# Query and key projections of the first attention as three fp16 products instead of one fp32 product

## The reference

```
x = x + attn(layernorm(x))                  # B=2, S=1024, E=128, H=16, D=64
Q = x @ Wq[h] + bq ; K = x @ Wk[h] + bk     # 128 columns a head: two halves of 64
V = x @ Wv[h] + bv                          # 64 columns a head
A1 = Q1 K1^T / 8 ; A2 = Q2 K2^T / 8         # 1024 x 1024, two of them a head
P  = softmax(A1) - lam * softmax(A2)
O  = P V ; Y = concat(O) @ Wo + bo ; Y = layernorm(Y) * gamma + beta, times 0.2
```

## Time and profile before

| what | value |
|---|---|
| median of 3 runs | 1667.67 us (1665.87 to 1667.73) |
| the profiled execution | 1667.55 us, span of its core 1665.8 us |
| TensorE matmul busy | 1543.7 us, 93% of the span |
| VectorE busy | 1316.4 us, 79% |
| ScalarE busy | 1266.0 us, 76% |
| GpSimd busy | 976.0 us, 59% |

### The profile page before, as it was taken

How to read it: one execution, slowest core, us unless ns; L and a number is a source line. 1 busy time by engine, 2 the same in 40 slices (tenths; PEclk the granted TensorE clock), 3 DMA queues, 4 the chain that set the end, 5 groups by cost and what they waited for, 6 DMA issues and landing times.

```text
span 1665.8 us, 27976 instructions
## 1 busy us (share of the span) xinstructions
PE 1543.7 (93%) x10479; PEld 641.2 (38%) x10479; DVE 1316.4 (79%) x2043; ACT 1266.0 (76%) x2039; POOL 976.0 (59%) x655
## 2 busy tenths in 40 slices
PE   5899999999999999999999999997575999999985
PEld 2444444444444444444444444434452222222223
DVE  6687887778877787878877788778958989999946
ACT  4788888888888888888888888884531888888872
POOL 2798887888878888788888888782022000111111
PEclk9999999999999999999999999998777999999997
DMA  4010011100111011110111111100001110000001
GB/s 125 20 34 24 22 28 25 37 23 23 28 34 28 24 26 25 34 26 23 29 23 34 28 23 26 26 19 6 1 12 29 27 34 15 16 15 16 15 15 32
DMA packets 51055, 43.67 MB, mean 26 GB/s; under 512 B 26101, under 2 KB 39322, under 8 KB 50922
## 3 DMA queue, kind: packets, MB, share of 16 engines
q1 hardware_dynamic: 50922, 41.90, 10.2%
HBM read 20.27 MB, written 1.31 MB: 13 GB/s over the span
## 4 chain that ended last, share of the span: by engine, by line
PE 76%; issue 9%; DVE 8%; ACT 4%; POOL 2%; DMA 1%; SPq 1%; POOLq 0%; ACTq 0%; DVEq 0%
PE PS L1500 22%; PE PS L1512 17%; PE PS L1524 14%; PE PS L1885 4%; PE PS L1567 4%; PE PS L1548 3%; PE PS L1848 2%; PE PS L1869 2%; PE PS L1584 2%; PE PS L1538 2%; DVE mxp L1406 2%; ACT ering L998 1%; ACT ering L786 1%; PE PS L1898 1%; POOL on L703 1%
## 5 line engine op out<-in xcount | busy, mean ns | idle before, releaser
L1091 DVE TENSOR_REDUCE nmx<-PS 128x1 f32<-128x1024 f32 x512 | 622.0, 1220 | 181.9 <-PE PS L1501 181.6
L606 POOL TENSOR_TENSOR ering<-ering 128x1024 f32<-128x1024 f32 x256 | 604.0, 2359 | 21.3
L786 ACT ACTIVATE ering<-PS,nmx 128x1024 f32<-128x1024 f32 x512 | 570.4, 1114 | 47.2 <-DVE nmx L1091 46.0
L1500 PE MATMUL PS<-region 64*128 64x512 f16 x1536 | 404.9, 381 | 7.2 <-DMA region<-region 5.3
L604 POOL TENSOR_SCALAR ering<-ering,rho 128x1024 f32<-128x1024 f32 x256 | 287.6, 1123 | 203.0 <-DVE rho L1100 200.5
L1501 PE MATMUL PS<-region 64*128 64x512 f16 x1536 | 404.9, 381 | 0.0
L1512 PE MATMUL PS<-ident,ering 128*128 128x128 f32 x2048 | 335.0, 286 | 8.8 <-ACT t L797 6.4
L1406 DVE TENSOR_REDUCE mxp<-PS 128x2 f32<-128x1024 f32 x256 | 304.1, 1221 | 41.7 <-PE PS L1869 38.1
L998 ACT ACTIVATE ering<-PS 128x1024 f32<-128x1024 f32 x256 | 260.4, 1025 | 74.2 <-PE PS L1848 66.6
L1512 PEld LDWEIGHTS PS<-ident,ering 128*128 128x128 f32 x2048 | 215.6, 141 | 260.7 <-issue 222.7
L1500 PEld LDWEIGHTS PS<-region 64*128 64x128 f16 x1536 | 112.6, 94 | 250.4 <-ACT ering L786 73.0
(11 more groups left out here) (289 smaller groups left out, 1800.1 us busy)
## 6 DMA issues: line engine op xcount, KB each, us to landing
region<-region SPq DMA_DIRECT2D x64, 256.0 KB, 3.5
osb<-scr SPq DMA_DIRECT2D x32, 128.0 KB, 3.1
rcp<-scr SPq DMA_DIRECT2D x32, 128.0 KB, 3.1
rcp<-scr SPq DMA_DIRECT2D x64, 64.0 KB, 2.0
region<-region SPq DMA_DIRECT2D x9, 128.0 KB, 2.6
x<-in_L_attn_X SPq DMA_DIRECT2D x4, 256.0 KB, 3.3
wq_raw<-in_L_attn_Wq SPq DMA_DIRECT2D x16, 64.0 KB, 3.2
wk_s<-in_L_attn_Wk SPq DMA_DIRECT2D x16, 64.0 KB, 1.9
```

The costliest lines, as they stand in the source:

```text
L606: P.tensor_tensor(e1, e1, e2, ALU.subtract).then_inc(s_sub_ok, 1)
L786: A.activation((E1, E2)[p][s % 4], PS[:, bank:bank + 2, :].rearrange("p a b -> p (a b)"), ACT.Exp, bias=nmx[:, 2 * s + p:2 * s + p + 1], s ...
L1091: V.tensor_reduce(nmx[:, 2 * s + p:2 * s + p + 1], PS[:, bank:bank + 2, :].rearrange("p a b -> p (a b)"), AX.X, ALU.max, negate=True).then ...
L1500: MM(PS[:, bank, :], top[0:64, ql, q], KT[b][0:64, p, kl, :], start=(j == 0), stop=(j == 2))
```

## The change

From the second head on (turn index `m >= 2`), Q and K are projected as three fp16 products (high x high, weights high x tokens low, weights low x tokens high) summed in PSUM, instead of one fp32 product. GpSimd makes the parts: of the transposed tokens once, in slots 1 to 4 of turn 0 (`part_x`), and of both weight matrices once a head (`part_w`), in slot 4 of every even turn, where `scale_q` now goes too (it was in slot 6). TensorE waits for the parts (`s_wlo_ok`, `s_xlo_ok`). The load of the next `wk_s` waits for the parts instead of for TensorE's products, from the second load on. Turns 0 and 1 are projected as before.

```diff
+        xs = sb("xs", [128, 2, N], F16)
+        wqh, wkh = [r16(15360 + 256 * i, 256).rearrange("p (l c) -> p l c", l=2) for i in range(2)]
...
+        PRODUCTS = ((0, 0), (0, 1), (1, 0))
...
                 if own and b == 0 and h + 1 < H0:
-                    sp.wait_ge(s_k0_mm, 2 * (n + 2))
+                    if h == 0:
+                        sp.wait_ge(s_k0_mm, 2 * (n + 2))
+                    else:
+                        sp.wait_ge(s_wlo_ok, h)
                     sp.dma_start(wk_s[:, :], a["L0_attn_Wk"][h + 1]).then_inc(s_ld_wk, 16)
...
+            def part_w(h):
+
+                scale_q(h)
+                pool.wait_ge(s_wqs_ok, h + 1)
+                pool.wait_ge(s_ld_wk, 16 * (h + 1))
+                pool.wait_ge(s_k0_mm, 4 * h)
+                P.tensor_copy(wqh[:, 0, :], wq_s[:, :])
+                P.tensor_copy(wkh[:, 0, :], wk_s[:, :]).then_inc(s_whi_ok, 1)
+                pool.wait_ge(s_whi_ok, h)
+                P.tensor_tensor(wqh[:, 1, :], wq_s[:, :], wqh[:, 0, :], ALU.subtract)
+                P.tensor_tensor(wkh[:, 1, :], wk_s[:, :], wkh[:, 0, :], ALU.subtract).then_inc(s_wlo_ok, 1)
+
+            def part_x(i):
+
+                at = slice(HF * i, HF * i + HF)
+                pool.wait_ge(s_xt_ev, i + 1)
+                P.tensor_copy(xs[:, 0, at], xT[:, at]).then_inc(s_xhi_ok, 1)
+                pool.wait_ge(s_xhi_ok, i + 1)
+                P.tensor_tensor(xs[:, 1, at], xT[:, at], xs[:, 0, at], ALU.subtract).then_inc(s_xlo_ok, 1)
...
             def prepare(n, s):
 
+                if n == 0 and 1 <= s < 5:
+                    part_x(s - 1)
...
-                    if s == 6 and b == 0 and h + 1 < H0:
-                        scale_q(h + 1)
+                    if s == 4 and b == 0 and h + 1 < H0:
+                        part_w(h + 1)
...
             def project_q(m):
 
-                pe.wait_ge(s_wqs_ok, m // 2 + 1)
+                if m < 2:
+                    pe.wait_ge(s_wqs_ok, 1)
+                else:
+                    pe.wait_ge(s_wlo_ok, m // 2)
+                    pe.wait_ge(s_xlo_ok, 4)
                 if m >= 1:
                     pe.wait_ge(s_exp, 16 * (m - 1) + 3)
                 for i in range(2):
-                    at = m % 2 * T + i * HF
-                    mm = MM(PS[:, Q_PAIR + i, :], wq_s[:, :], xT[:, at:at + HF], start=True, stop=True)
+                    at = slice(m % 2 * T + i * HF, m % 2 * T + i * HF + HF)
+                    dst = PS[:, Q_PAIR + i, :]
+                    if m < 2:
+                        mm = MM(dst, wq_s[:, :], xT[:, at], start=True, stop=True)
+                        continue
+                    for j, (wl, xl) in enumerate(PRODUCTS):
+                        mm = MM(dst, wqh[:, wl, :], xs[:, xl, at], start=(j == 0), stop=(j == 2))
                 mm.then_inc(s_q_mm, 1)
 
             def project_k(m, part):
 
-                pe.wait_ge(s_ld_wk, 16 * (m // 2 + 1))
+                if m < 2:
+                    pe.wait_ge(s_ld_wk, 16)
+                else:
+                    pe.wait_ge(s_wlo_ok, m // 2)
+                    pe.wait_ge(s_xlo_ok, 4)
...
-                for c in range(2):
-                    at = m % 2 * T + c * HF
-                    mm = MM(dst[64 * c:64 * c + 64, :], wk_s[:, 64 * part:64 * part + 64], xT[:, at:at + HF],
-                            start=True, stop=True)
+                d = slice(64 * part, 64 * part + 64)
+                for j, (wl, xl) in enumerate(PRODUCTS[0:1] if m < 2 else PRODUCTS):
+                    for c in range(2):
+                        at = slice(m % 2 * T + c * HF, m % 2 * T + c * HF + HF)
+                        if m < 2:
+                            mm = MM(dst[64 * c:64 * c + 64, :], wk_s[:, d], xT[:, at], start=True, stop=True)
+                        else:
+                            mm = MM(dst[64 * c:64 * c + 64, :], wkh[:, wl, d], xs[:, xl, at], start=(j == 0),
+                                    stop=(j == 2))
                 mm.then_inc(s_k0_mm, 1)
```

More of the change, by code:

```diff
@@ L190, in two_layers @@
         s_wqs_ok = sem("s_wqs_ok")
+        s_whi_ok = sem("s_whi_ok")
+        s_wlo_ok = sem("s_wlo_ok")
+        s_xhi_ok = sem("s_xhi_ok")
+        s_xlo_ok = sem("s_xlo_ok")
         s_fill = sem("s_fill")
@@ L1498, in scores @@
                 q = slice(s * 128, s * 128 + 128)
-                for j, (ql, kl) in enumerate(((0, 0), (0, 1), (1, 0))):
+                for j, (ql, kl) in enumerate(PRODUCTS):
                     MM(PS[:, bank, :], top[0:64, ql, q], KT[b][0:64, p, kl, :], start=(j == 0), stop=(j == 2))
```

## The result

The changed kernel took 1642.88 us (median of 4 runs, 1640.82 to 1644.57) against 1667.7 before: a ratio of 0.9849, 95% interval 0.9829 to 0.9868. In three later comparisons, each with its own runs of the kernel before, the same kernel took 1644.04, 1644.45 and 1645.10 us, ratios 0.9866 (0.9853 to 0.9880), 0.9885 (0.9870 to 0.9899) and 0.9866 (0.9851 to 0.9882). So the gain is 19 to 25 us, and the first median the lowest of four; the forecast of 20.1 lies in that span, and the three later medians lie inside the range. The turns say more than the medians: their length repeats within 0.02 us.

A forecast was written before the change was run, and what follows sets the result against it. TensorE was taken to bound the kernel. A turn loses 0.26 (second K product) + 0.41 (Q) = 0.67 us; 30 turns give 20.1 us, so 1667.55 - 20.1 = 1647.4 us, range 1643 to 1654.

The forecast's parts named there:

- the first K product: K's first half in slot 0: its 0.26 us saving becomes a wait for VectorE, so worth nothing.
- GpSimd at nothing: Making the parts delays tile 5 by 1.2 us with 2.1 us to spare, so costs nothing.
- rival (a): The first K product counts too, VectorE's chain moving with it: 27.9 us saved, 1639.7 us; chance 0.09.
- The second K product: K's second half, after the wait for VectorE: fp16 saves 0.26 us a turn, counted in full.
- Q: Q's projection as six fp16 passes, 1.40 us instead of 1.81: saves 0.41 us a turn, counted in full.
- rival (c): Weight loads no longer hide behind the shorter fp16 passes: turns 0.14 us longer, 1671.8 us; chance 0.05.
- The cap at 0.74: A turn cannot lose more than about 0.74 us, where ScalarE's chain alone sets the pace.
- SyncE at nothing: The next K weights load earlier and no longer hold the swap of Q; effect nothing.
- (b): Only Q counts; VectorE's and ScalarE's chain takes the second K product's gain: 12.3 us saved, 1655.3 us; chance 0.07.
- (d): GpSimd's fp16 casts are several times dearer, each head pays 1.9 us: 28 against 20.1 us, 1676 us; chance 0.03.

The follow-up runs named there:

- e3: Changed kernel with only the first half of K projected in fp32 again; 1642.71 us, turns of 33.70 us.
- e14: Changed kernel with the addition to the output cut to 16 columns and the first half of K in fp32 again; 1644.02 us, turns of 33.70 us.
- e13: Changed kernel with the addition to the output cut to 16 columns, first half of K left in fp16; 1640.91 us, turns of 33.53 us.
- e5: Changed kernel with only the second half of K projected in fp32 again; 1648.41 us, turns of 33.85 us.
- e4: Changed kernel with only Q projected in fp32 again; 1654.44 us, turns of 34.03 us.
- e8: Changed kernel with V also projected as three fp16 products, from the second pair of heads on; 1644.55 us, turns of 33.61 us.
- e2: Changed kernel with GpSimd making all parts but TensorE projecting in fp32; 1663.28 us, ratio 0.9984 against the kernel before, turns of 34.36 us.
- e6: Changed kernel with the third product of Q (low part of its weights) left out; 1635.09 us, turns of 33.42 us.

## Why the prediction was wrong, and where it was right

The step that failed is the one that put the first K product at nothing. It gave 0.09 us a turn, 2.7 us of the 4.7 by which the forecast was short. The rest of the working held: two of three terms to within 0.03 us, and GpSimd at nothing.

- **The first K product: 0.00 forecast, 0.09 us measured** (33.61 against 33.70 with it in fp32). What was wrong is the sentence that VectorE runs without a gap from 517.77 to its low part of K. It read end against start: these are the two rows of before between them.

```profile
518.91 1.21 DVE L1133 TENSOR_TENSOR yT<-yT,PS 128x1024 f32<-128x1024 f32 x1
520.12 1.23 DVE L1091 TENSOR_REDUCE nmx<-PS 128x1 f32<-128x1024 f32 x1
```

518.91 + 1.21 = 520.12 looks seamless. But the same pair in the profile after stands closer:

```profile
507.68 1.22 DVE L1124 TENSOR_REDUCE nmx<-PS 128x1 f32<-128x1024 f32 x1 [0.56 <-PE PS L1534]
508.83 1.21 DVE L1166 TENSOR_TENSOR yT<-yT,PS 128x1024 f32<-128x1024 f32 x1
509.95 1.22 DVE L1124 TENSOR_REDUCE nmx<-PS 128x1 f32<-128x1024 f32 x1
511.09 0.74 DVE L1138 SCALAR_TENSOR_TENSOR region<-PS,small,region 128x512 f16<-128x512 f32 x1
```

The maximum starts 1.12 us after the addition. The recorded 1.21 us reach 0.09 into the next instruction, so there was an idle of 0.09 us before 520.12, and TensorE held it: a maximum starts 0.86 us after its score when TensorE releases it (516.91 to 517.77 in the earlier trace rows), and 519.26 + 0.86 is 520.12. With the product back in fp32 both distances return (e3, 1.21 and 0.86), and with the addition cut short the profile names TensorE as the releaser of that maximum, again at 0.86 (e14). Thus the first 0.09 us that the K product gives count, then the addition on VectorE holds (the chain of 5.15 us), and without it, after 0.15, ScalarE's copy (5.09 us; e13 and e14). "Perfetto Trace Analysis" in the Trainium skill, section Optimizing Scalar/DVE Operations, says that a profiled latency contains a write acknowledgement that overlaps with the next instruction; with 1.12 against 1.21 us the trace agrees. The 0.09 itself comes from the rows alone: had I compared starts, rival (a) would have had its way and its size.
- **The second K product: 0.26 forecast, 0.23 measured in the rows and 0.24 in the turn.** The score group was a good stand-in for three fp16 pairs; on tile 128*64 they take 0.78 instead of 0.75 us. It counts in full (e5).
- **Q: 0.41 forecast, 0.42 measured,** in full (e4). Six passes with a load each follow at (1.39 - 0.10) / 6 = 0.215 us: rival (c) is excluded. "TensorE: Matmul & The Clock Gate" in the Trainium skill, section The mechanism, says that a load overlaps a running matmul only on another row group; the trace does not agree: all passes use the same rows, and they follow at 0.215 us here and at 0.056 us in e8, with a load of 0.098 us each. The same section also says that a load into the background weight buffer is pulled ahead of running matmuls, and that would fit.
- **Sum of a turn:** 0.09 + 0.24 + 0.42 = 0.75 by the turns of e3, e5 and e4, and 34.36 (e2) less 33.61 is 0.75 as well. Times 30, the 0.76 of the kernel before and after is 22.8 us. With 0.67 I had 20.1.
- **The cap at 0.74** named the right place, score (3, 0) behind ScalarE's exponential, but no rows of the prediction give its size: 527.57 - 526.98 = 0.59 and at most 0.10 back at the transposes make 0.69. The same failed step is in it: that chain starts at an exponential which VectorE releases, so it moved forward with VectorE. I had score (3, 0) at 526.98 - 516.91 = 10.07 us after the second score of slot 0, and it came at 9.98. Behind it another 0.16 can be won (e6), so the turn could lose 0.95. With the cap at 0.74 the forecast also contradicted its own rival (a), which asked for 0.93 a turn.
- **GpSimd and SyncE at nothing:** right for GpSimd; parts alone leave the turn at 34.36 (e2). SyncE's earlier load was not tested alone, since e2 keeps the old wait beside the new one; but the three TensorE terms leave at most 0.01 us of the turn for it. Rivals (b) and (d) are excluded by e5 and e2.
- **The range.** It left 0.12 us out. Its low end took only a part of (a), as if a product counted or didn't. The intermediate value, up to the next chain, stood in none of my cases. With it the sum would have been 1667.55 - 22.8 = 1644.8, inside the range and near the three later medians; so the other 2 us of the first 24.8 are no step of the prediction. In the first profile the span is 26.8 us shorter: 21.9 in 29 turns, 1.1 ahead of them and 3.8 behind the loop, where profiles of the same kernel scatter by 3 us each. The three later comparisons gave 19 to 22 us by their ratios. The cause of the scatter was not traced.

## What to carry to other kernels

An engine that seems to run without a gap may still be released by another one: compare the distance between starts with that of the same pair elsewhere, and the lag behind the supposed releaser with its usual value, before an edit is costed at nothing. A saving in front of a chain that is nearly bound counts up to the second chain, so forecast a part of it. Three fp16 products for one fp32 product give TensorE nearly a fourth of its time back at 512 columns (1.39 us for 1.81) and at 128 (0.67 for 0.89), but the kernel gets it only where no other engine's release stands right behind: in slot 7 it got none.

## What was not expected of the hardware

- fp16 passes of 128 columns on the whole array follow at 0.056 us, about a quarter of the 0.215 of 512 columns, although each has a weight load of 0.098 us of its own (e8): the loads overlap each other and the passes.
- GpSimd's casts from fp32 to fp16 cost what a scaling in fp32 does: 289 to 294 ns against 298 ns for 128x128.
- A difference of 2.9 us outside the loop's turns (e2) for a kernel whose turns are unchanged; not explained.
